# A hybrid layer on one core: state-space tiles in rounds, two feed-forward PSUM banks, one table of shares a step

## The reference, cut to what matters

```python
def mixer(x):                               # state space, 8 heads, state 64 x 64
    z, xs, B, C, dt = split(x @ W_in)       # 512, 512, 64, 64, 8 columns
    dt = softplus(dt + dt_bias); decay = exp(-exp(A_log) * dt)
    h = 0
    for t in range(512):                    # done in blocks of 128 tokens
        h = decay[t] * rotate(h, dt[t]) + dt[t] * outer(B[t], xs[t])
        y[t] = C[t] @ h
    y = (y + D_skip * xs) * silu(z)
    return (y * rsqrt(mean(y*y) + 1e-5) * norm_weight) @ W_out

def delta(x):                               # delta rule, 8 heads of 32
    q, k, v, beta = x @ Wq, unit(x @ Wk), silu(x @ Wv), sigmoid(x @ Wb)
    for t in range(512):
        S += beta[t] * outer(k[t], v[t] - k[t] @ S)
        o[t] = q[t] @ S
    return layernorm(o) * ln_w + ln_b

def ffn(x):                                 # ternary weights, 1024 hidden
    h = silu(x @ w1.T * s1) * (x @ w2.T * s2)
    h = gelu(h @ h1.T * sh1); h = gelu(h @ h2.T * sh2)
    return h @ w3.T * s3

x += mixer(norm(x)); x += ffn(norm(x)); x += delta(norm(x)); x += ffn(norm(x))
```

## Time and profile before

| what | us |
|---|---|
| median of 3 runs (3175.0 to 3180.48) | 3176.88 |
| the profiled execution's own time | 3179.42 |
| its span | 3177.4 |

### The profile page before, as it was taken

How to read it: one execution, slowest core, us unless ns; L and a number is a source line. 1 busy time by engine, 2 the same in 40 slices (tenths; PEclk the granted TensorE clock), 3 DMA queues, 4 the chain that set the end, 5 groups by cost and what they waited for, 6 DMA issues and landing times.

```text
span 3177.4 us, 54420 instructions
## 1 busy us (share of the span) xinstructions
PE 2491.4 (78%) x20928; PEld 2195.7 (69%) x20928; DVE 1483.2 (47%) x3604; ACT 1157.8 (36%) x2426; POOL 926.0 (29%) x1216
## 2 busy tenths in 40 slices
PE   4678868888688886888868888678877888777688
PEld 3567757777577775787657776568766777666578
DVE  3434553445534445444454444545444444544541
ACT  2235432445225442245412544134432354323223
POOL 2123323233223232233323223232322233233233
PEclk7679988999799997999979998789987999898799
DMA  6000000000000000000000000000000000000000
GB/s 202 1 1 1 3 12 15 1 1 18 19 7 1 1 18 21 4 1 1 20 21 3 1 8 21 14 1 1 15 14 14 1 1 10 12 15 6 21 10 7
DMA packets 86976, 43.33 MB, mean 14 GB/s; under 512 B 71472, under 2 KB 81584, under 8 KB 86704
## 3 DMA queue, kind: packets, MB, share of 16 engines
q1 hardware_dynamic: 83040, 28.12, 3.5%
q0 software_dynamic: 3664, 11.53, 1.1%
HBM read 27.05 MB, written 12.58 MB: 12 GB/s over the span
## 4 chain that ended last, share of the span: by engine, by line
PE 46%; DVE 25%; ACT 10%; issue 10%; POOL 5%; DMA 3%; SPq 1%; DVEq 0%; POOLq 0%; ACTq 0%
PE F L1218 21%; DVE prod L1079 4%; DVE ti L1081 3%; PE Q L1261 3%; PE F L1240 2%; PE Q L1329 2%; PE Q L1346 2%; PE Q L1308 2%; POOL hA_lo L580 2%; DVE hid L899 2%; PE Q L1444 2%; PE Q L1414 1%; PE Q L1381 1%; PE Q L1300 1%; PE Q L1312 1%
## 5 line engine op out<-in xcount | busy, mean ns | idle before, releaser
L1218 PE MATMUL F<-hA_hi,h_sb 128*128 128x256 f32 x2048 | 568.1, 311 | 107.8 <-POOL hA_lo L580 107.4
L580 POOL TENSOR_TENSOR hA_lo<-hid,hA_hi 128x256 fp32r<-128x256 f32 (+1 forms) x384 | 353.0, 920 | 879.2 <-ACT hA_hi L706 494.0
L1218 PE MATMUL F<-hA_lo,h_sb 128*128 128x256 f32 x2048 | 542.9, 299 | 0.0
L1218 PE MATMUL F<-hB_hi,h_sb 128*128 128x256 f32 x2048 | 526.1, 295 | 0.3
L1218 PEld LDWEIGHTS F<-hA_hi,h_sb 128*128 128x128 f32 x2048 | 426.6, 208 | 127.9 <-POOL hA_lo L580 115.4
L1218 PE MATMUL F<-hB_lo,h_sb 128*128 128x256 f32 x2048 | 508.8, 287 | 0.0
L1198 PE MATMUL F<-xf_hi,w_sb 128*128 128x256 f32 x1024 | 319.0, 338 | 162.6 <-DVEq L902 69.2
L1218 PEld LDWEIGHTS F<-hA_lo,h_sb 128*128 128x128 f32 x2048 | 428.3, 209 | 0.5
L1218 PEld LDWEIGHTS F<-hB_hi,h_sb 128*128 128x128 f32 x2048 | 400.8, 196 | 19.0 <-issue 15.3
L1218 PEld LDWEIGHTS F<-hB_lo,h_sb 128*128 128x128 f32 x2048 | 401.7, 196 | 0.3
L1198 PEld LDWEIGHTS F<-xf_hi,w_sb 128*128 128x128 f32 x1024 | 234.9, 229 | 183.8 <-DVEq L902 82.9
(11 more groups left out here) (212 smaller groups left out, 4492.7 us busy)
## 6 DMA issues: line engine op xcount, KB each, us to landing
h_sb<-h_dram POOLq DMA_DIRECT2D x2, 4096.0 KB, 24.5
x_sb<-x_dram SPq DMA_DIRECT2D x8, 512.0 KB, 3.9
a_scr<-q_sb SPq DMA_DIRECT2D x128, 32.0 KB, 1.7
au<-a_scr SPq DMA_DIRECT2D x8, 512.0 KB, 3.2
t_scr<-ti SPq DMA_DIRECT2D x8, 512.0 KB, 3.0
tbd<-t_scr SPq DMA_DIRECT2D x128, 32.0 KB, 1.9
out_dram<-x_sb SPq DMA_DIRECT2D x8, 512.0 KB, 3.3
w_sb<-w_dram POOLq DMA_DIRECT2D x3, 1024.0 KB, 9.0
```

The lines of the kernel that those rows point to most:

```text
L580: pool.tensor_tensor(lo, hid[:, n % 2, 0:w, :], hi.bitcast(F32), ALU.subtract).then_inc(f_lo.handle, 1)
L1218: last = pe.matmul(ps[:, i * TOK:(i + 1) * TOK], w[:, k, o:o + P], part[:, k, :], start=(i == 0 and k == 0 and part is src[0]), stop=(i == ...
```

## The change

1. **Rounds.** `ssm_stage` runs 5 rounds of 9 steps. Round r holds the front of tile r (input, projection, softplus, sums, angles, sine and cosine, decays, `seg`, its sums of logs and, last, their exponents) and the back of tile c = r-1 (transposes of `hat`, scores, y, state, output). Round 0 is a front alone, round 4 a back alone. What both need at once is doubled (`sz`, `dta`, `decays` by r % 2), and the rotation uses `ang` and `angk` as scratch in place of `y` and `yT`. New signals: `a_projd`, `a_bc`, `a_dta`.
2. **Banks.** The feed-forward has two PSUM banks (FB = 2), the attention six (Q[0] to Q[5]). y, its transpose and the output product stand in Q[5], `hat` and the scores in Q[3] and Q[4].
3. **Plans.** The delta stage and the state-space stage of an iteration are now one window (`joined`), with 4 units that are dealt over its steps by one table. The passes are shifted by a unit: an iteration takes the second unit of the last pass of the iteration before (`rest`) and then three fresh ones. The iteration b = 1 stands ahead of the loop with 3 units, and the two delta windows after it take 3 and 2. Norms of the two kinds of pass have separate halves (`fmv2`, `frstd2`).
4. **SP.** Store and load of x stand after the first group of `tbd` loads of a delta stage.

Matmuls of the feed-forward that the tables place on PE, counted from the plans (transposes of a unit's input included):

| stage | iteration before | iteration now | b = 1 now | first delta window after the loop | second |
|---|---|---|---|---|---|
| D1 | 288 | 436 | 372 | 420 | 364 |
| inverse | 124 | 224 | 128 | 224 | 88 |
| way through DRAM | 24 | 36 | 32 | 32 | 32 |
| D2 | 276 | 160 | 164 | 392 | 228 |
| state space | 712 | 568 | 372 | - | - |

The 568 are 64, 116, 128, 128 and 132 in the five rounds; the 372 are 32, 80, 80, 80 and 100. The state space of batch 1 has 712 before and now. The two windows after the loop have 712 each before.

```diff
-SSM_STEPS = 8
+SSM_STEPS = 9
...
+FB = 2
+UNIT = [(1, 1.0)] * KT + [(0.5, 2.0)] * (2 * KT) + [(1, 0.5)] + [(0.5, 2.0)] * 2
+D2_END = D20 + D2_STEPS * NT
+SSM_END = SSM_STEPS * (NT + 1)
...
-SSM_PLAN = spread([1, 5.9, 8.7, 3, 2, 3, 1, 0] * NT)
-DELTA_PLAN = spread([2.8, 4, 2, 2, 1] * NT + [0.5] * 8 + [0.5] * (SUB_STEPS - 9) + [6]
-                    + [2, 1] + ([1.2, 1.2] * NB + [2]) * NT)
-assert sum(SSM_PLAN) == sum(DELTA_PLAN) == UNITS * SLICES
+def shares(d1, inverse, gap, d2):
+    return ([v * d1 / (11.8 * NT) for v in (2.8, 4, 2, 2, 1)] * NT + [inverse / 10]
+            + [inverse * 0.9 / (SUB_STEPS - 1)] * (SUB_STEPS - 1) + [gap / 2] * 2 + [d2 / (D2_STEPS * NT)] * (D2_STEPS * NT))
+def ssm_shares(whole):
+    return [v * whole / 44 for v in [1, 1, 0, 0, 1, 0, 1, 0, 0] + [1, 1, 1, 1, 1, 1, 1, 1, 1] * (NT - 1)
+            + [0, 0, 2, 2, 0, 2, 0, 2, 2]]
+FIRST_PLAN = spread(ssm_shares(89), UNITS)
+PEEL_PLAN = spread(shares(45, 15, 4, 20) + ssm_shares(49.5), 3)
+BODY_PLAN = spread(shares(52.5, 28, 4, 20) + ssm_shares(73.5), 4)
+LATE_PLAN = spread(shares(52.5, 28, 4, 49), 3)
+LAST_PLAN = spread(shares(45, 12, 3, 29), 2)
 PI = 3.141592653589793
...
+def joined(*stages):
+    base = 0
+    for stage, first, count in stages:
+        for position in stage:
+            yield base + position - first
+        base += count
 def window(attention, ffn, plan):
...
-        F = [ctx.enter_context(nc.psum_tensor(f"F{i}", [P, 512], F32)) for i in range(4)]
-        Q = [ctx.enter_context(nc.psum_tensor(f"Q{i}", [P, 512], F32)) for i in range(4)]
+        F = [ctx.enter_context(nc.psum_tensor(f"F{i}", [P, 512], F32)) for i in range(FB)]
...
+                def next_batch():
+                    store(b - 2)
+                    sp.wait_ge(x_loaded.handle, x_loaded.at(b, 16))
+                    sp.wait_ge(x_stored.handle, x_stored.at(b - 2, 16))
+                    load(b + 1)
+                delta(b - 1, next_batch)
+            delta(B - 2, lambda: store(B - 3))
             delta(B - 1)
...
+                for r in range(NT + 1):
+                    c = r - 1
...
+                        yield SSM_STEPS * r + 2
...
+                        yield SSM_STEPS * r + 3
+                        act.wait_ge(a_proj.handle, a_proj.at(b, r + 1))
+                        if r:
...
+                        yield SSM_STEPS * r + 4
+                        act.wait_ge(a_ang.handle, a_ang.at(b, r + 1))
...
+                        yield SSM_STEPS * r + 5.5
+                        act.wait_ge(a_yv.handle, a_yv.at(b, c + 1))
...
+                            act.wait_ge(a_out.handle, a_out.at(b, c))
...
+                        yield SSM_STEPS * r + 8
+                        act.wait_ge(a_segp.handle, a_segp.at(b, r + 1))
...
+                                       scale=-1.0).then_inc(a_exp.handle, 1)
...
+                for r in range(NT + 1):
+                    c = r - 1
+                    if r:
+                        yield SSM_STEPS * r + 1
+                        dve.wait_ge(a_hatT.handle, a_hatT.at(b, c + 1))
...
+                    if r < NT:
...
+                        yield SSM_STEPS * r + 3
+                        dve.wait_ge(a_score.handle, a_score.at(b, c + 1))
+                        dve.wait_ge(a_exp.handle, a_exp.at(b, c + 1))
...
+                        dve.wait_ge(a_soft.handle, a_soft.at(b, r + 1))
...
+                        yield SSM_STEPS * r + 4
...
+                        yield SSM_STEPS * r + 5
...
+                        dve.wait_ge(a_y.handle, a_y.at(b, c + 1))
...
+                        yield SSM_STEPS * r + 6
+                        dve.wait_ge(a_dta.handle, a_dta.at(b, r + 1))
+                        dve.tensor_tensor(seg[:], bcast(stri[:], 1, H), bcast(dta[:, r % 2, 1, :], 2, P),
...
+                        if r + 1 < NT:
...
+                for r in range(NT + 1):
+                    c = r - 1
+                    if r < NT:
+                        yield SSM_STEPS * r
+                        pe.wait_ge(a_xn.handle, a_xn.at(b, r + 1))
+                        if r:
+                            pe.wait_ge(a_sumc.handle, a_sumc.at(b, r))
...
+                        last.then_inc(a_xTp.handle, 1)
+                    if r:
+                        yield SSM_STEPS * r + 1
+                        pe.wait_ge(a_hat.handle, a_hat.at(b, c + 1))
+                        pe.wait_ge(a_flat.handle, a_flat.at(b, c + 1))
...
+                        last.then_inc(a_hatT.handle, 1)
+                    if r < NT:
+                        yield SSM_STEPS * r + 1.5
+                        pe.wait_ge(a_xT.handle, a_xT.at(b, r + 1))
+                        if r:
+                            pe.wait_ge(a_exp.handle, a_exp.at(b, r))
+                        for q, c0, c1, done in ((0, 2 * DI, W_IN, a_projd), (2, DI, 2 * DI, None), (1, 0, DI, a_proj)):
...
+                                last.then_inc(done.handle, 1)
+                    if r:
+                        yield SSM_STEPS * r + 3
+                        pe.wait_ge(a_bT.handle, a_bT.at(b, c + 1))
+                        pe.wait_ge(a_cT.handle, a_cT.at(b, c + 1))
...
+                        last.then_inc(a_score.handle, 1)
+                    if r < NT:
+                        yield SSM_STEPS * r + 4
+                        pe.wait_ge(a_dta.handle, a_dta.at(b, r + 1))
+                        pe.wait_ge(a_bc.handle, a_bc.at(b, r + 1))
...
+                    if r:
+                        yield SSM_STEPS * r + 5
+                        pe.wait_ge(a_pm.handle, a_pm.at(b, c + 1))
+                        pe.wait_ge(a_wx.handle, a_wx.at(b, c + 1))
...
+                            pe.wait_ge(a_res.handle, a_res.at(b, c))
...
+                        last.then_inc(a_y.handle, 1)
+                    if r < NT:
+                        yield SSM_STEPS * r + 6
+                        pe.wait_ge(a_seg.handle, a_seg.at(b, r + 1))
+                        pe.wait_ge(a_zx.handle, a_zx.at(b, r + 1))
...
+                        last.then_inc(a_segp.handle, 1)
+                    if r:
+                        yield SSM_STEPS * r + 7
+                        pe.wait_ge(a_yv.handle, a_yv.at(b, c + 1))
...
+                        last.then_inc(a_yTp.handle, 1)
+                        yield SSM_STEPS * r + 8
+                        pe.wait_ge(a_yT.handle, a_yT.at(b, c + 1))
...
+                        last.then_inc(a_out.handle, 1)
...
             pe.wait_ge(wd_dma, 16)
-            window(ssm_stage(1, 1), ffn(0, 0), SSM_PLAN)
-            with pe.Fori(1, B - 1) as b:
-                window(delta_stage(b - 1, 2 * b), ffn(2 * b - 1, b), DELTA_PLAN)
-                window(ssm_stage(b + 1, 2 * b + 1), ffn(2 * b, b - 1), SSM_PLAN)
-            window(delta_stage(B - 2, 2 * B - 2, False), ffn(2 * B - 3, B - 1), DELTA_PLAN)
-            window(delta_stage(B - 1, 2 * B - 1, False), ffn(2 * B - 2, B - 2), DELTA_PLAN)
-            alone(ffn(2 * B - 1, B - 1, False))
+            window(ssm_stage(1, 1), ffn(0, 0), FIRST_PLAN)
+            def attention(b):
+                return joined((delta_stage(b - 1, 2 * b), 0, D2_END), (ssm_stage(b + 1, 2 * b + 1), 0, SSM_END))
+            def fresh(b):
+                return [(ffn(2 * b - 1, b), 0, 2 * SLICES), (ffn(2 * b, b - 1, units=(0,)), 0, SLICES)]
+            def rest(b):
+                return (ffn(2 * b - 2, b - 2, units=(1,)), SLICES, SLICES)
+            window(attention(1), joined(*fresh(1)), PEEL_PLAN)
+            with pe.Fori(2, B - 1) as b:
+                window(attention(b), joined(rest(b), *fresh(b)), BODY_PLAN)
+            b = B - 1
+            window(delta_stage(b - 1, 2 * b, False), joined(rest(b), (ffn(2 * b - 1, b), 0, 2 * SLICES)), LATE_PLAN)
+            window(delta_stage(b, 2 * b + 1, False), ffn(2 * b, b - 1), LAST_PLAN)
+            alone(ffn(2 * b + 1, b, False))
```

533 lines of the change are left out of this document (267 added, 266 removed).

## The result

| | before | after |
|---|---|---|
| median of the runs, us | 3176.88 (3175.0 to 3180.48) | 3288.03 (3287.79 to 3288.83) |
| profiled span, us | 3177.4 | 3286.0 |
| mean granted clock | 0.891 | 0.852 |

After over before is 1.0349, 95% interval 1.0325 to 1.0372. I forecast 2965, in a range of 2830 to 3110. The changed kernel is slower, and its time lies outside the range.

A forecast was written before the change was run, and what follows sets the result against it. PE is used most, but stages are chains over four engines with idle gaps (inverse: DVE-bound). An iteration falls from 385.7 to 353.5 us; the program's terms sum to -211 from 3179.4, less 2.5 for the median: 2965, range 2830 to 3110.

The forecast's parts named there:

- 164 forecast: State-space stage of a loop iteration: five rounds, 106 + 6 + 24 + 28 = 164 us, against 187.6 before.
- Some 16 matmuls stand there, 2 us, so 3.4 are left: Middle round: PE's wait for `seg` behind y and state update, 5.4 us, covered by 2, leaving 3.4.
- 58 forecast: D2 of a loop iteration: 71.2 - 16.2 + 3 = 58 us, bounds 53 and 66.
- 116 fewer at 0.14: D2: 116 feed-forward matmuls taken out at 0.14 us each save 16.2 us.
- 86 forecast: D1 of a loop iteration: 76.5 + 18.5 - 9 = 86 us, with 148 matmuls more.
- I let half be filled, 6: D1: of 12.5 us of PE idle time, added feed-forward matmuls fill half, 6 us.
- (D): Rival: slower, since with two banks PE stands 6 us behind feed-forward drains; 3255 us, chance 0.08.
- My bound of 95: D1: upper bound of 95 us, if none of its idle time is filled.
- The other two marks: Forecast wrong if the state-space stage stays above 180 us, or waits for DVE's and ACT's drains of F exceed 200.
- 31 forecast: Inverse of a loop iteration: drain waits go, PE and DVE run beside each other, 31 us against 35.7.
- late `tbd` loads: D2: if the second group of `tbd` loads is late, D2 pays up to 5 us once an iteration.
- (B): Rival: rounds don't shorten the chain on in-order engines; middle round 43 us, stage 188, whole 3105, chance 0.19.

The follow-up runs named there:

- e7: Changed kernel, in a round DVE makes the next tile's `seg` before the y chain instead of after it: 3164.4 us, ratio to before 0.996.
- e2: Kernel before (four banks, no rounds), delta-window slices dealt 43 / 22 / 4 / 20 to D1, inverse, DRAM way, D2: 3290.5 us, ratio 1.0357.
- e14: Changed kernel with odd tables in the last two delta windows, leaving stages there with almost no or no feed-forward filler: 3317.05 us, ratio 1.0431.
- e9: e7's kernel with the loop's table moving w3, xT and eight w1/w2 slices into the DRAM way, D2 keeping h slices: 3169.64 us, ratio 0.9969.
- e1: Kernel before with two feed-forward PSUM banks instead of four and nothing else: 3207.77 us, ratio 1.0092.
- e6: Changed kernel with two unused bf16 matmuls of 512 columns added to each of D2's 16 chunks: 3306.98 us, ratio 1.0398.

## Why the prediction was wrong

**The state-space stage: 164 forecast, 175.9 measured.** The step that failed: "Some 16 matmuls stand there, 2 us, so 3.4 are left". I had read the chain from the lone tile, where no drain stands between the state update and `seg`, and took 5.4 us for it. With feed-forward work beside it the two drains come between, and PE stood 4 to 6 us. The wait itself was sized nearly right (15.9 us for four, 4.0 each; forecast 3.4). What I put at nothing is the price of a matmul when PE stands: I took 65.4 us for the attention and 0.125 for each of the 568, 136.4 us, and PE was busy 145.4, at a mean clock of 0.86 where the rows I read had 0.94. That is 9 of the 12 us; the other 3 are idle time. One moved instruction (e7) brings the stage to 158.2, under the forecast. Of the 323 us between forecast and result, 124 go by it.

**D2: 58 forecast, 79.2 measured, the largest error, 21 us an iteration.** Two steps failed. "116 fewer at 0.14" took the matmuls' busy time off the stage and kept the price of a full clock for the rest. The busy time went from 62.5 to 60.9 us and not to 46: 156 matmuls cost 0.191 each at a mean clock of 0.74, and the attention's own 33.5 us in place of 27.3. That is 15 of the 21 us; idle time, 18.3 where the sum had 11.7, is the rest. e2, with h slices and four banks, gives 0.03 for each matmul taken out. No run came below 67 us with as many matmuls, and D2 with none at all took 58.7 (e14). And I priced slices by number, not by kind: the eight w1/w2 slices that the new table puts into D2 bring some 20 more instructions to DVE, which is half of D2's chain. e9 takes them away, and 11 us with them. I had weighed the kind for the inverse and for round 2, but never asked which slices D2 gets. How much of the loss is the clock and how much DVE's queue, the runs don't separate.

**D1: 86 forecast, 96.8 measured.** "I let half be filled, 6" failed: idle time went from 12.5 to 12.6. The waits for the chain did shrink, from 14.5 to 4.6 us, but 9.0 us of waits for a bank that DVE drains came in their place. That is rival (D)'s mechanism, and the sum for D1 had no term for it. Whether four banks would keep the gain isn't tested: e2's D1, with four banks and 380 matmuls, has no such wait and is idle 11.6 us all the same. The records also have 176 more matmuls where the table has 148. My bound of 95 for "none filled" was the nearest case, and the mark I had set for being wrong (past 95) was met. The other two marks were not: the state-space stage is under 180 us, and PE's waits for drains of F are 117 us in the program.

**Inverse: 31 forecast, 34.9 measured.** The waits for drains did go, as forecast. But DVE's 62 operations became longer, 31.7 us in place of 27.2 (last section). **DRAM way:** 14.5 and 16.2, right within 2. The late `tbd` loads that I gave up to 5 us don't show in D2.

**The other parts.** The lone stage gained 30.5 us (first dt operation of batch 1 at 160.2, before at 190.7), I had 11: rounds are 27 us where I took 34, by a PE share that I thought large. The stretch of batch 1 came out 10 longer (forecast 2), the iteration b = 1 377 (331), the two late stages +37 and +9 (+17, -6), the last pass +3 (+3). These repeat the errors of D1, D2 and the `seg` wait.

**The rivals.** (D), slower by two banks, had the sign and 0.08. Its mechanism is real and was oversized: 29 us alone (e1), and in the changed kernel the wait for a bank that DVE drains went from 69.2 us to 105.5. The longest of these 44 waits is 6.0 us, as I had it, but the mean is 2.4. In D1 they are most of the idle time. The rule of the Trainium skill, Perfetto Trace Analysis, section Matmuls, on rotating through different PSUM banks agrees with e1 in sign. (B), rounds don't shorten the chain, named the cause in general: "a front's wait now holds back a neighbour's back". I put 3105 on it, because I kept the forecast's D1 and D2 beside it. The true outcome was B in the rounds together with linear prices failing in D1 and D2. The range, whose slow end held just one of these errors, was too narrow.

## What to carry to other kernels

When work of two tiles is interleaved on in-order engines, list for each engine what stands between an operation's operands and the operation, with the filler's drains in it. Here a 1.2 us operation could have run 6 us before its turn in the round shown, and moving it up was worth 124 us. Price a stage's filler from the same stage at two loads, with the granted clock of both beside it: taking filler out of D2 saved 0.03 to 0.06 us a matmul, where its busy time had been 0.14. Look at what ends each wait and not only at their sum: D1's stayed, and its cause changed. Deal slices by which engine drains them and not by their number alone, and expect that a gain in one stage is taken back by the place the slices move to (e9).

## What the runs showed of the hardware

These two-input operations of DVE and POOL's low parts hold each other up when they overlap. DVE by line in the inverse, first in the changed kernel, then in e14 where POOL is idle:

```profile
L1183 DVE TENSOR_TENSOR prod<-ti,au 128x31 f32<-128x31 f32 (+15 forms) x31 | 17.9, 578 | 7.1 <-DMA au<-a_scr 6.1
L1185 DVE TENSOR_TENSOR ti<-ti,prod 128x31 f32<-128x31 f32 (+15 forms) x31 | 13.8, 444 | 1.1
```

```profile
L1183 DVE TENSOR_TENSOR prod<-ti,au 128x31 f32<-128x31 f32 (+15 forms) x31 | 14.0, 451 | 6.9 <-DMA au<-a_scr 5.9
L1185 DVE TENSOR_TENSOR ti<-ti,prod 128x31 f32<-128x31 f32 (+15 forms) x31 | 10.6, 343 | 1.1
```

The same 62 operations take 31.7 us beside 8.7 us of busy POOL, and 24.6 us beside next to none (0.08): the difference, 7.1, is most of POOL's time. The kernel before lies between, 27.2 us beside 4.7. One of them in the changed kernel's timeline, with its neighbours:

```profile
1228.37 0.45 DVE L1183 TENSOR_TENSOR prod<-ti,au 128x156 f32<-128x156 f32 x1
...
1229.18 1.29 POOL L617 TENSOR_TENSOR hB_lo<-hid,hB_hi 128x512 fp32r<-128x512 f32 x1 [2.45 <-ACT hB_hi L763]
1229.21 1.59 DVE L1183 TENSOR_TENSOR prod<-ti,au 128x175 f32<-128x175 f32 x1
...
1231.22 0.53 DVE L1183 TENSOR_TENSOR prod<-ti,au 128x192 f32<-128x192 f32 x1
```

The operation of 175 columns takes 1.59 us between one of 156 at 0.45 and one of 192 at 0.53; it starts 0.03 us behind POOL's and ends 0.33 us after it. So each h slice beside the inverse costs the chain up to the time of the low part that POOL makes for it, though DVE has nothing to do with that slice. The Trainium skill, SBUF — State Buffer, section Who interferes with whom, states an exclusive lock on a port pair that DVE and GpSimd share, and the rows agree with it. I had applied it to the rounds and forgotten it in the inverse, where it takes back my 4 us.

And the clock: the same state-space matmuls cost 145.4 us of busy time at a granted clock of 0.86 and 134.9 at 0.94 (e7), and the 156 feed-forward matmuls of D2 29.8 us at 0.74 and 26.7 at 0.87 (e6). e7's stage became shorter by the first difference and more. In e6 the stage did not, with the dummies in it.
